# Weight loads moved to ScalarE's queue, and the weights' scaling moved within the first slots, in a cross-attention and coupling kernel

## The reference

```python
q, k, v = heads(layernorm(x)), heads(ctx), heads(ctx)          # 16 heads of 16
u = einsum('hbqd,hbkd->hbqk', q, k) * scale / sqrt(16)
logits = where(mask, -inf, tanh(u) * exp(log_C))
x = x + merge(softmax(logits) @ v) @ W_out.T

f = layernorm(x)
gf = global_net(mean over tokens of f)                         # 3 small layers, gelu, sigmoid
out = f
for _ in range(3):
    tf = coupling_net(out)       # 256-256-128-64-1, exact gelu, sigmoid at the end
    c = 0.1 + adaptive_range * (0.7 * gf + 0.3 * tf - 0.5) * 2
    out = out + c * twist(out)   # quarters (a,b,p,q) -> (p,-q,-a,b)
x = x + out
```

## Time and profile before

| | us |
|---|---|
| median of 3 executions | 1055.38 |
| lowest and highest | 1054.36 and 1056.46 |
| the profiled execution's own time | 1054.31 |
| its span, first to last instruction | 1052.5 |
| busy: TensorE / VectorE / ScalarE / GpSimd | 972.9 / 814.1 / 902.9 / 606.9 |

### The profile page before, as it was taken

The page is one execution under the profiler, slowest core; times in us unless marked ns, Lnnn a source line. Parts: engine busy times, 40 slices in busy tenths (PEclk is TensorE's granted clock), DMA queues, the critical chain, the costliest instruction groups (busy, mean ns, idle before and its releaser), DMA issues.

```text
span 1052.5 us, 21763 instructions
## 1 busy us (share of the span) xinstructions
PE 972.9 (92%) x7260; PEld 528.3 (50%) x7260; DVE 814.1 (77%) x1655; ACT 902.9 (86%) x1121; POOL 606.9 (58%) x1077
## 2 busy tenths in 40 slices
PE   5899999999999999999999999999999999997894
PEld 4556435564355544555445653556435654464431
DVE  3889785996868876887859978599686897687475
ACT  3999888997899978998789987899789997896575
POOL 3366715887069850898328981588705986077304
PEclk7999999999999999999999999999999999999997
DMA  5433001430024300332005310153002330021002
GB/s 119 90 60 60 6 2 34 113 86 6 2 70 91 79 1 1 90 90 59 2 1 120 90 30 1 27 113 92 9 2 69 91 79 1 1 46 41 11 1 81
DMA packets 191117, 51.70 MB, mean 49 GB/s; under 512 B 165920, under 2 KB 174624, under 8 KB 191008
## 3 DMA queue, kind: packets, MB, share of 16 engines
q1 hardware_dynamic: 191008, 50.31, 22.5%
HBM read 33.37 MB, written 16.78 MB: 48 GB/s over the span
## 4 chain that ended last, share of the span: by engine, by line
PE 41%; ACT 24%; POOL 12%; issue 10%; DVE 10%; SPq 2%; DMA 0%; POOLq 0%; ACTq 0%; DVEq 0%
PE ps L1299 11%; ACT probs L939 10%; ACT probs L945 9%; PE ps L1283 7%; PE ps L1186 5%; PE ps L1267 4%; PE ps L1308 4%; PE ps L1217 2%; PE ps L1202 2%; POOL f_hat L479 2%; DVE move_u L802 2%; DVE move_v L804 2%; ACT f_t L955 2%; DVE f_t L808 2%; POOL rstd L469 1%
## 5 line engine op out<-in xcount | busy, mean ns | idle before, releaser
L939 ACT ACTIVATE probs<-ps,u_scale 120x2048 f32<-120x2048 f32 x128 | 254.4, 1988 | 24.0 <-PE ps L1186 24.0
L945 ACT ACTIVATE probs<-probs,exp_bias,clip 120x2048 f32<-120x2048 f32 x128 | 271.4, 2120 | 0.1
L1299 PE MATMUL ps<-h,w 128*128 128x512 f32 x384 | 186.9, 609 | 1.6 <-ACT h L973 1.6
L1186 PE MATMUL ps<-q_t,k_t 32*120 32x256 f32 x2048 | 147.9, 402 | 19.1 <-ACT probs L939 18.2
L717 DVE STREAM_TRANSPOSE o_t<-ps 128x512 f32<-128x512 f32 x128 | 90.6, 708 | 73.7 <-PE ps L1202 73.4
L1217 PE MATMUL ps<-wo_t,of_t 128*128 128x256 f32 x512 | 143.6, 403 | 1.5 <-DVE xy L742 1.4
L1202 PE MATMUL ps<-probs,va 120*32 120x256 f32 x2048 | 138.8, 389 | 1.6 <-ACT probs L945 1.0
L498 POOL TENSOR_SCALAR tok_c<-tok_c,c_tok 128x32 f32<-128x32 f32 x8 | 2.3, 286 | 237.5 <-issue 237.5
L1186 PEld LDWEIGHTS ps<-q_t,k_t 32*120 32x120 f32 x2048 | 93.4, 179 | 58.2 <-issue 53.7
L973 ACT ACTIVATE h<-f_t,b 128x512 f32<-128x512 f32 x144 | 96.9, 718 | 18.0 <-DVE f_t L827 13.5
L1217 PEld LDWEIGHTS ps<-wo_t,of_t 128*128 128x128 f32 x512 | 86.9, 189 | 50.7 <-issue 42.2
(11 more groups left out here) (138 smaller groups left out, 1770.4 us busy)
## 6 DMA issues: line engine op xcount, KB each, us to landing
xy<-in_x_dram SPq DMA_DIRECT2D x64, 256.0 KB, 3.3
out_dram<-xy SPq DMA_DIRECT2D x64, 256.0 KB, 2.0
cbuf<-in_ctx_dram SPq DMA_DIRECT2D x64, 120.0 KB, 2.8
va<-in_ctx_dram SPq DMA_DIRECT2D x64, 120.0 KB, 3.6
tok_c<-coup SPq DMA_DIRECT2D x256, 0.5 KB, 2.0
move_v<-in_L_xattn_W_out_dram SPq DMA_DIRECT2D x1, 256.0 KB, 5.3
move_u<-in_L_ffn_cn_w_dram SPq DMA_DIRECT2D x1, 256.0 KB, 3.3
w<-in_L_ffn_cn_w_dram SPq DMA_DIRECT2D x1, 128.0 KB, 3.1
```

The costliest lines, as they stand in the source:

```text
L939: eng.activation(probs[:, b % 2, n * HALF:(n + 1) * HALF, :].rearrange("k h q -> k (h q)"), banks(SCORE_BANK, 4)[0:KEYS, :], ACT.Tanh, sca ...
L945: eng.activation(p, p, ACT.Exp, scale=clip[0:KEYS, 0:1], bias=exp_bias[:, b:b + 1]).then_inc(s_exp, 1)
L1186: last = eng.matmul(banks(SCORE_BANK + r)[0:KEYS, odd * S:(odd + 1) * S], k_t[rows, b % 2, odd, n, :], q_t[rows, b % 2, n, :], start=True, ...
L1299: last = eng.matmul(banks(bank), w2[:, k, :], h1[:, p % 2, k, :], start=(k == 0), stop=(k == EK - 1))
```

## The change

The 19 loads of `weight_loads` leave SyncE's program and become the first instructions of ScalarE's. Six instead of ten identity products are run. In slot 0, exp(0, 0) stands before tanh(0, 1) instead of behind it. The transposed maxima and the spread value go to `SIDE_BANK`, which the first slots do not use otherwise. `project(0, 0)` waits for N_WO (W_out's transposed copy is made) instead of N_SPREAD. On TensorE the spread product stands behind scores(2, 0) and values(1, 0) instead of ahead of them, and on VectorE the split stands at the back of slot 2 instead of at its front.

```diff
--- before.py
+++ after.py
@@ -408,8 +408,6 @@
                     load(1)
                     load(2)
                     load_values(0)
-                    for dst, src in weight_loads:
-                        eng.dma_start(dst, src).then_inc(s_w, 16)
                 elif 0 <= i + 4 < NB and i >= -1 and not after_ffn(i):
                     load(i + 4)
                 for b in late[:1]:
@@ -662,11 +660,11 @@
 
             def largest_weight():
                 eng.wait_ge(s_pe0, 3)
-                eng.tensor_reduce(w_row[:], banks(X_BANK)[0:1, 0:P], AX.X, ALU.max).then_inc(s_vec0, 1)
+                eng.tensor_reduce(w_row[:], banks(SIDE_BANK)[0:1, 0:P], AX.X, ALU.max).then_inc(s_vec0, 1)
 
             def split_weights():
                 eng.wait_ge(s_pe0, 4)
-                eng.tensor_scalar(w_max[:], banks(X_BANK)[:, 0:1], TINY, None, ALU.max).then_inc(s_vec0, 1)
+                eng.tensor_scalar(w_max[:], banks(SIDE_BANK)[:, 0:1], TINY, None, ALU.max).then_inc(s_vec0, 1)
                 eng.wait_ge(s_vec0, N_SPREAD)
                 eng.reciprocal(w_inv[:], w_max[:]).then_inc(s_vec0, 1)
                 eng.tensor_scalar(uv_scale[:], w_max[:], 1.0 / (F_SCALE * W_SCALE), None, ALU.mult).then_inc(s_vec0, 1)
@@ -855,8 +853,6 @@
 
             late = []
             for kind, i in slots():
-                if i == 2 and kind == "attention":
-                    split_weights()
                 if kind == "attention":
                     new, nxt, here, old = ahead_in_slot(i), i + 1, i - 1, i - 2
                     if i == -2:
@@ -894,6 +890,8 @@
                     if i == 1:
                         largest_weight()
                         coupling_constants()
+                    if i == 2:
+                        split_weights()
                 else:
 
                     for m in range(EK):
@@ -929,6 +927,8 @@
 
         @block.scalar
         def _(eng):
+            for dst, src in weight_loads:
+                eng.dma_start(dst, src).then_inc(s_w, 16)
             eng.wait_ge(s_scal, 32)
             eng.activation(clip[:], scal[:, 1:2], ACT.Exp).then_inc(s_act0, 1)
 
@@ -1037,9 +1037,11 @@
                         tanh(i, 0)
                     if 0 <= i - 1 < NB and not first:
                         exp(i - 1, 1)
+                    if i == 0:
+                        exp(i, 0)
                     if 0 <= i < NB and not first:
                         tanh(i, 1)
-                    if 0 <= i < NB:
+                    if 0 < i < NB:
                         exp(i, 0)
                     if 0 <= i - LAG < NB:
                         features(i - LAG)
@@ -1122,7 +1124,7 @@
             eng.wait_ge(s_pool0, 3)
             eng.wait_ge(s_vec0, N_MASK)
             eng.transpose(banks(TR_BANK)[0:KEYS, 0:NB], mask_f[:], ident[0:NB, 0:NB]).then_inc(s_pe0, 1)
-            for _ in range(10):
+            for _ in range(6):
                 eng.matmul(banks(X_BANK)[:, 0:P], ident[:], ident[:], start=True, stop=True)
 
             def transpose_w_out():
@@ -1137,13 +1139,13 @@
 
                 eng.wait_ge(s_vec0, N_MAX)
                 eng.wait_ge(s_vec0, N_WO)
-                eng.transpose(banks(X_BANK)[0:1, 0:P], w_max[:], ident[:]).then_inc(s_pe0, 1)
+                eng.transpose(banks(SIDE_BANK)[0:1, 0:P], w_max[:], ident[:]).then_inc(s_pe0, 1)
 
             def largest_spread():
 
                 eng.wait_ge(s_pool0, 7)
                 eng.wait_ge(s_vec0, N_ROW)
-                eng.matmul(banks(X_BANK)[:, 0:1], ones[0:1, :], w_row[:], start=True, stop=True).then_inc(s_pe0, 1)
+                eng.matmul(banks(SIDE_BANK)[:, 0:1], ones[0:1, :], w_row[:], start=True, stop=True).then_inc(s_pe0, 1)
 
             def queries(b):
 
@@ -1208,7 +1210,7 @@
                 eng.wait_ge(s_oft, b + 1)
                 if t == 0:
                     if b == 0:
-                        eng.wait_ge(s_vec0, N_SPREAD)
+                        eng.wait_ge(s_vec0, N_WO)
                     else:
                         eng.wait_ge(s_y, b)
                     if after_ffn(b + 2):
@@ -1359,13 +1361,13 @@
             for kind, i in slots():
                 if kind == "attention":
                     nxt, here, old = i + 1, i - 1, i - 2
-                    if i == 2:
-                        largest_spread()
                     if i != early:
                         if 0 <= i < NB:
                             scores(i, 0)
                         if 0 <= here < NB:
                             weighted_values(here, 0)
+                        if i == 2:
+                            largest_spread()
                         if 0 <= nxt < NB:
                             queries(nxt)
                         if place(i) in SIDE_PRODUCTS:
```

## The result

The changed kernel takes 1059.63 us (median of 5 executions, 1058.81 to 1060.38) against 1055.38 (5 executions, 1054.36 to 1056.66): +4.25 us, ratio 1.0039, 95% interval 1.0028 to 1.0051. It is slower, and the interval lies clear of 0.2%. The profiled execution took 1058.81 us, with a span of 1056.9.

The account below looks back on a forecast made before the run. It took ScalarE's own queue to bound the first attention stage, gap-free from 50.50 us on. +6.5 (issues) - 3.25 (earlier weights) + 0.65 (split) = +3.9 us on 1055.38 gave 1059.3 us, range 1053 to 1063.

Parts of the forecast that it names:

- part 1: Weight loads on ScalarE's queue: their issues delay `clip` from 6.93 to 13.45 us, +6.5 us; net +3.25 at the third tanh.
- the bound of 11.0: Earliest start of `clip` in us, if no stall is met and the table load goes ahead of the issues.
- From `clip` to the first tanh: Start of slot 0: 6.7 us, the same as the 6.69 before, so the first tanh comes at 20.15, +6.5 us.
- What it gives back: Slots 0 to 1: weights land earlier, so first to third tanh takes 7.86 us instead of 11.14, gain 3.3 us.
- Part 2: Four identity products fewer on TensorE: up to 1.4 us if `clip` stayed at 6.93, nothing behind 13.45.
- Part 3: Exponential before slot 0's second tanh: third tanh does not move at the low clock; 0.5 us worse at the high one.
- Part 4: Spread product and split moved: 2.35 us ahead at slot 3's tanh, given back in slot 3; 0.65 us worse at slot 4.
- t + 27.1: Forecast time of slot 4's tanh, t being the third tanh; t + 26.45 in the kernel before.
- The sum: At slot 4's tanh: +6.5 - 3.25 + 0.65 = +3.9 us, all of it reaching the end.
- Rival A: ScalarE issues at 0.2 us each, so `clip` stays where its input lands: -3.6 us, 1051.8; chance 0.14.
- Rival B: Issues cost as forecast but the split hides, slot 4's tanh at t + 23.8: +0.6 us, 1056.0; 0.22 including a variant.
- Rival C: Queues hinder each other, every values load stalls ScalarE's issues, `clip` at 16.9: +7.3 us, 1062.7; chance 0.16.

Follow-up runs that it names:

- e5: Changed kernel with 8 single-column loads on ScalarE's queue ahead of `clip`, the other 11 on SyncE's; 1056.83 us against 1055.93 for the kernel before, ratio 0.9999.
- e8: Changed kernel with 18 identity products instead of 6; 1060.58 us, ratio 1.0045 to the kernel before.
- e2: Changed kernel with the 19 weight loads back on SyncE's queue, all other edits kept; 1056.44 us, ratio 1.0014 to the kernel before.
- e7: Changed kernel with the second tanh of slot 0 ahead of the first exponential again; 1060.73 us, ratio 1.0046 to the kernel before.
- e4: Changed kernel with VectorE's split in five pieces, four ahead of the keys copies of slots 2 to 5; 1055.11 us, ratio 1.0008 to the kernel before.

## Why the prediction was right, and where it was not

It named the sign, the mechanisms and a time of 1059.3, and 1059.63 was measured. The mechanisms were right; that the time came within 0.4 us is in part luck, since three terms were too small by 2.4 us together and the medians show some 2 us less than the start lost. Point by point:

- **The issues (part 1).** 19 issues and `clip` at 13.45 were forecast; the issues ended at 12.98 and `clip` started at 14.31. The term was 0.8 us too small: 12.25 us of issues where I had 11.45, nearly the 12.59 that they took on SyncE's queue with its stall. SyncE was held as well, 4.9 us on the load of x behind its first values. The order with the table load behind the issues was right (the row at 13.01, right ahead of `clip`), and the bound of 11.0 was not in play. The Trainium skill ("ScalarE: Activation LUTs", Step-by-step: what each stage is for) places the table load right before the activation that needs it, and the trace agrees. Sharing the issues brought SyncE's last weight issue forward from 18.51 to 14.86 us in e5; what stands behind issues pays for them, `clip` 7.4 us in the changed kernel. The Trainium skill ("DMA: Bandwidth & Descriptors", Issuing engines are not separate DMA queues) says that a second issuing engine saves only the time of starting the transfers, and e5 agrees with that.
- **From `clip` to the first tanh.** 6.7 forecast, 6.57 measured, with the score products at 2.08 us. Two readings on the way were off without changing the sum: the queries at 9.18 were not at the full clock (1.05 us, 1.09 in the changed kernel, 0.63 in e8), and the work of 15 to 20 us is denser than the idle time it was set beside, not thinner.
- **What it gives back.** From first to third tanh 7.86 was taken as the middle of 7.24 and 8.49 or so. The traces of the changed kernel show 8.49, 7.55 and 7.56: the upper end and two values near the middle. The third tanh was forecast at 28.0, measured at 29.37, 27.89 and 28.44.
- **Part 2, fewer identity products:** nothing, as forecast. e2 shows the 1.2 us that they win if `clip` is early.
- **Part 3, the swap:** nothing (e7), at the lower clock's pace.
- **Part 4, the split.** The gain of slots 1 and 2 came as forecast: the tanh of slot 3 lies 15.40 us behind the third (15.7 forecast, 18.05 before). VectorE's split ended at t + 21.16 (t + 21.5 forecast). What was mis-sized is what follows: "it is 4.25, so t + 27.1". That took the products behind the keys at the full clock. After the pause of 2.80 us ahead of them, which I had foreseen, the granted clock was 0.71 and 0.50, and the products took up to twice as long: from the keys to the tanh of slot 4 it was 5.62, 7.07 and 6.76 us in the three traces instead of 4.25. That gives t + 28.1 to 29.6, so 1.7 to 3.1 us worse than before instead of 0.65.
- **The sum.** At slot 4 it was +3.9 forecast and +6.3 measured. In the first trace the parts of the difference are 0.7 up to the first tanh, 0.6 from there to the third and 1.0 in slot 3 (up to 2.5 in the other traces). That the median comes so close to the forecast owes something to the scatter of the end, which the prediction did not have: "so all of it reaches the end" holds only within about 2 us. The bounds that the prediction lists add up to 1053.0 and 1064.2, not 1063. Rival A, fast issues, is out: the 19 issues of the changed kernel lie between 0.45 and 1.20 us. Rival B (the split hides) is out; it would hide if it were spread (e4). Rival C did not come about (`clip` at 14.31, not 16.9), though its +7.3 lies nearer to the +6.3 at slot 4 than the forecast's +3.9 does.

## What to carry to other kernels

An engine's queue is a line: transfers put at its head delay whatever it computes first, by all of their issues. Count the issues against the time at which that first instruction's input lands, and put there only as many as fit (8 of 19 here); the rest stayed on the queue that had them. A block of side work belongs cut up into the gaps that the engine has in each slot, not at the back of one slot; with about one microsecond free per slot, 3.8 us in one piece cost 4.3 to 5.8 us against the spread version (28.1 to 29.6 against 23.8 from the third tanh to slot 4), since TensorE, stopped for 2.8 us, then ran its products at up to twice their time. The pieces have a deadline too: the last one, in slot 5, came 0.9 us late for its first reader.

## What the runs showed of the hardware

- The granted clock in the records is not always what the products show. In the changed kernel's trace it reads 1.00 from 15 to 20 us, while the 16 score products that start at 18.68 take 2.08 us, as at 0.50 in the earlier trace rows:

```profile
15.00:20.00 5.00, 3.04 (x18) 2.25 (x22) 2.32 (x7) 0.00 (x0) 2.24 (x5) 1.00 0.56 101
```

- The 19 issues take 0.65 us each on average on ScalarE's queue (12.25 / 19), and the two shown with the result, for a matrix of 256 KB and for a value spread over a column, 0.48 us both. The 19 lie between 0.45 and 1.20 us, the longest being that of a single column: the size of the transfer does not set the price of its issue.
- With the weights issued at once, a load of 512 bytes (log_C), issued at 2.92 us (2.94 before), was there at 9.5 instead of 6.9, and x(0)'s statistics began at 6.04 instead of 4.27.
